# Transposes ahead of the stage borders, stage 3's and 9's preparations too, and adds from VectorE to GpSimd in stage 10, in a twelve-stage perceiver kernel

## What is computed

```python
# stages 3 and 9 (L1_xattn with biases and a mask, L3_xattn without)
qh, kh, vh = proj(q, Wq, bq), proj(k, Wk, bk), proj(v, Wv, bv)   # 16 heads of 8
scores = jnp.where(mask, einsum('bhqd,bhkd->bhqk', qh, kh) / np.sqrt(8), -1e9)
out = einsum('bhqk,bhkd->bhqd', softmax(scores), vh)             # 257 keys
return einsum('bsd,ed->bse', out, Wo) + bo
# stage 8 (L2_ffn): 32 experts x 4 sets, one token of the 32 picked per set
perm = (logits == max(logits, axis=-3))
inner = relu(einsum('bnesd,esdf->bnesf', permuted, W1) + b1)
result_permuted = einsum('bnesf,esdf->bnesd', inner, W2) + b2
# stage 10 (L3_attn): dense 16-head attention and top-6 sparse attention, fused
fused = sig * dense_output + (1.0 - sig) * sparse_output
x = layernorm(src + fused, ln1_g, ln1_b)
ff = relu(x @ ff1_w.T + ff1_b) @ ff2_w.T + ff2_b
return layernorm(x + ff, ln2_g, ln2_b)
```

## Time and profile before

| | |
|---|---|
| runs | 2987.17, 2988.69, 2990.55 (median 2988.69) |
| the profiled execution's own time | 2988.34 |
| its span | 2986.6 |
| mean granted clock | 0.958 |
| busy: PE, DVE, ACT, POOL | 2773.4, 1757.0, 1308.3, 706.8 |
| borders 2 to 3, 8 to 9, 9 to 10, 10 to 11 | 807.8, 1515.6, 1768.8, 1937.7 |

### The profile page before, as it was taken

How to read it: one execution, slowest core, us unless ns; L and a number is a source line. 1 busy time by engine, 2 the same in 40 slices (tenths; PEclk the granted TensorE clock), 3 DMA queues, 4 the chain that set the end, 5 groups by cost and what they waited for, 6 DMA issues and landing times.

```text
span 2986.6 us, 69018 instructions
## 1 busy us (share of the span) xinstructions
PE 2773.4 (93%) x26509; PEld 1781.9 (60%) x26509; DVE 1757.0 (59%) x5682; ACT 1308.3 (44%) x3510; POOL 706.8 (24%) x1552
## 2 busy tenths in 40 slices
PE   8999998997999979998699987699999999999898
PEld 7888885565577756665467755444444444444465
DVE  6787777766478867559568867712232232232544
ACT  4665565552288842358368864311121121111221
POOL 2444441000178830034037751000000000000000
PEclk9999999999999989869889999889999999999999
DMA  5111110000021100410021130030000000000000
GB/s 134 50 48 46 48 41 8 3 3 6 20 55 49 43 25 1 118 60 2 6 58 41 41 133 27 15 126 1 1 1 1 1 1 1 1 1 1 1 1 15
DMA packets 125903, 92.03 MB, mean 31 GB/s; under 512 B 41283, under 2 KB 122566, under 8 KB 124230
## 3 DMA queue, kind: packets, MB, share of 16 engines
q1 hardware_dynamic: 125574, 87.61, 10.3%
HBM read 83.89 MB, written 3.67 MB: 29 GB/s over the span
## 4 chain that ended last, share of the span: by engine, by line
PE 78%; DVE 10%; issue 5%; DVEq 3%; ACT 2%; POOLq 1%; POOL 1%; DMA 0%; SPq 0%; ACTq 0%
PE banks L3558 25%; PE banks L491 3%; PE banks L926 3%; PE banks L897 2%; PE banks L910 2%; PE banks L935 2%; PE banks L3981 2%; PE banks L3972 2%; PE banks L521 2%; PE banks L3970 2%; PE banks L500 2%; PE banks L471 2%; PE banks L508 2%; PE banks L509 2%; PE banks L1759 1%
## 5 line engine op out<-in xcount | busy, mean ns | idle before, releaser
L1011 ACT ACTIVATE probs<-probs,nbias 128x257 f32<-128x257 f32 x512 | 254.3, 501 | 0.0
L1227 POOL TENSOR_SCALAR probs<-probs,rinv 128x257 f32<-128x257 f32 x512 | 237.6, 483 | 25.0 <-DVE rinv L1109 21.8
L3558 PE MATMUL banks<-Wz,hT 128*64 128x256 f32 x2048 | 226.4, 379 | 0.0
L3831 POOL COPY rb<-hT 128x512 f32<-128x512 f32 x32 | 35.8, 1118 | 801.7 <-ACT hT L3634 777.4
L3558 PE MATMUL banks<-Wn,hT 128*64 128x512 f32 x1024 | 225.4, 593 | 0.0
L3558 PE MATMUL banks<-Wr,hT 128*64 128x512 f32 x1024 | 225.2, 592 | 0.0
L3558 PEld LDWEIGHTS banks<-Wz,hT 128*64 128x64 f32 x2048 | 147.0, 137 | 87.7 <-issue 18.3
L3800 DVE TENSOR_TENSOR pr<-hb,banks 128x512 f32<-128x512 f32 x32 | 22.0, 688 | 298.4 <-PE banks L3613 298.4
L717 POOL TENSOR_SCALAR probs<-probs,rinv 128x257 f32<-128x257 f32 x256 | 120.1, 482 | 205.0 <-DVE rinv L657 204.4
L3558 PEld LDWEIGHTS banks<-Wr,hT 128*64 128x64 f32 x1024 | 73.5, 137 | 132.6 <-issue 128.0
L3558 PEld LDWEIGHTS banks<-Wn,hT 128*64 128x64 f32 x1024 | 70.9, 137 | 129.5 <-issue 129.5
(11 more groups left out here) (664 smaller groups left out, 6485.0 us busy)
## 6 DMA issues: line engine op xcount, KB each, us to landing
kvT<-in_ctx_T SPq DMA_DIRECT2D x192, 128.5 KB
kv<-in_ctx SPq DMA_DIRECT2D x64, 128.0 KB
kv<-in_ctx SPq DMA_DIRECT2D x32, 256.0 KB
W<-in_L_ffn_W_T SPq DMA_DIRECT2D x2, 2048.0 KB
Wr<-in_L_ffn_w_hh_T SPq DMA_DIRECT2D x1, 4096.0 KB
Wn<-in_L_ffn_w_hh_T SPq DMA_DIRECT2D x1, 4096.0 KB
Wz<-in_L_ffn_w_hh_T SPq DMA_DIRECT2D x1, 4096.0 KB
v_last<-v_last SPq DMA_DIRECT2D x192, 8.0 KB, 1.6
```

Of the source, the lines that this page charges most:

```text
L1011: i = e.activation(s, s, ACT.Exp, bias=self.nbias[v][:, r:r + 1], scale=self.scale, accum_out=self.rows_sum[v][:, r:r + 1])
L1227: e.tensor_scalar(s, s, self.rinv[v][:, r:r + 1], 1.0, ALU.mult, ALU.mult)
L3558: mm = e.matmul(self.bank[b][hf * BATCH:(hf + 1) * BATCH, 0:n], lhs, rhs, start=start, stop=stop, tile_position=(0, hf * BATCH))
```

## The change

1. The transposes of quarters 0 to 2 and their yT copies go ahead of the barrier in stages 1 to 3 and 5 to 11, in new methods `pe_early` and `act_early`; quarter 3 stays behind it. Banks for them are chosen to be free.
2. Stages 3 and 9: SP issues the first mask and the first four contexts at the end of the previous stage's queue (`sp_early`); POOL makes masks, `wo_heads` (from DVE), `of_batch`, the maps of mask 0 and the last keys of batches 0 and 1 ahead of the barrier (`pool_early`). The products of the last row, keys and values of batches 0 and 1 and the four `v_rows` products with their copies (from DVE to ACT) become eight pieces k = 0 to 7 of `ahead_pe` and `ahead_act`. In stage 3 they stand in `pe_early`, around the transposes and the projection of tile 0. The prologue then runs scores(g - 2) ahead of keys and values g for g = 2 to 5.
3. Stage 9's eight pieces run among the experts of stage 8: PE's piece n // 2 on odd pairs n, in front of `expert_pe`, ACT's piece n // 2 - 2 on even pairs from 4 on. `keep_warm` in `expert_pe` goes.
4. Stage 10: `scale_rows` and `add_x` of every quarter but the last add run on POOL, with new counts x1_scaled, x1_normed and x1_added; DVE does the four softmaxes in a row, then the sparse top and rest. `last_add` fuses the last norm, gain and add.
5. Stage 11's `of_row` is made ahead of the barrier.

```diff
+    def pe_early(self, e):
+        self.norm_pe(e, (0, 1, 2))
+
+    def act_early(self, e):
+        self.norm_act_yT(e, (0, 1, 2))
...
+    def ahead_pe(self, e, k):
+        p, bank = self.prog, self.bank[2 + k % 2]
+        if k == 0:
+            p.constants_made.wait_ge(e, 1)
+            self.weights_wait(e)
+            e.matmul(bank[:, 0:BATCH], self.wk[:, :], self.ctx_last[:, :], start=True, stop=True)
+            e.matmul(bank[:, BATCH:2 * BATCH], self.wv[:, :], self.ctx_last[:, :], start=True, stop=True)
+            i = e.matmul(bank[0:1, P:2 * P], p.ones[0:1, 0:1], self.brow[:, :], start=True, stop=not self.biased)
+            if self.biased:
+                i = e.matmul(bank[0:1, P:2 * P], self.bv[:, :], self.wo[:, :], start=False, stop=True)
+            i.then_inc(self.prep_mm.up(), 1)
+        if k == 1:
+            self.keys_values(e, 0, bank)
+        if k == 2:
+            self.prep_act.wait_ge(e, 3)
+            e.matmul(bank[:, 0:P], p.ones[0:1, :], self.bo_eff[:, :], start=True, stop=True).then_inc(self.prep_mm.up(), 1)
+        if k == 3:
+            self.v_ready.wait_ge(e, 1)
+            self.keys_values(e, 1, bank)
+        if k >= 4:
+            self.wo_ready.wait_ge(e, 1)
+            self.prep_act.wait_ge(e, 4)
+            self.v_ready.wait_ge(e, 2 * (k % 2))
+            self.v_rows_ready.wait_ge(e, k - 5)
+            e.matmul(bank[0:BATCH, :], self.v_lastT[:, :], self.wo_heads[:, (k - 4) * 512:(k - 3) * 512],
+                     start=True, stop=True).then_inc(self.prep_mm.up(), 1)
+
+    def ahead_banks_free(self, e):
+        self.v_rows_ready.wait_ge(e, 4)
+
+    def pe_early(self, e):
+        before = self.prog.stages[self.index - 1]
+        self.x_free = None
+        if not before.RUNS_AHEAD:
+            self.ahead_pe(e, 0)
+            self.ahead_pe(e, 1)
+        self.norm_pe(e, (0, 1))
+        before.last_banks_free(e)
+        self.n_yT.wait_ge(e, 1)
+        self.project(e, 0)
+        self.norm_pe(e, (2,))
+        if not before.RUNS_AHEAD:
+            for k in range(2, 8):
+                self.ahead_pe(e, k)
     def pe(self, e):
-        p, bank = self.prog, self.bank
-        self.norm_pe(e, (0,))
-        self.weights_wait(e)
-        e.matmul(bank[4][:, 0:BATCH], self.wk[:, :], self.ctx_last[:, :], start=True, stop=True).then_inc(self.prep_mm.up(), 1)
-        e.matmul(bank[5][:, 0:BATCH], self.wv[:, :], self.ctx_last[:, :], start=True, stop=True).then_inc(self.prep_mm.up(), 1)
-        i = e.matmul(bank[6][0:1, 0:P], p.ones[0:1, 0:1], self.brow[:, :], start=True, stop=not self.biased)
-        if self.biased:
-            i = e.matmul(bank[6][0:1, 0:P], self.bv[:, :], self.wo[:, :], start=False, stop=True)
-        i.then_inc(self.prep_mm.up(), 1)
-        self.norm_pe(e, (1, 2))
-        self.x_free = None
-        self.n_yT.wait_ge(e, 1)
-        self.prep_act.wait_ge(e, 1)
-        self.project(e, 0)
-        self.prep_act.wait_ge(e, 3)
-        e.matmul(bank[7][:, 0:P], p.ones[0:1, :], self.bo_eff[:, :], start=True, stop=True).then_inc(self.prep_mm.up(), 1)
-        self.keys_values(e, 0)
-        self.norm_pe(e, (3,))
+        self.ahead_banks_free(e)
+        self.n_yT.wait_ge(e, 3)
+        self.prep_pool.wait_ge(e, 1)
+        for g in range(2, 6):
+            self.scores(e, g - 2)
+            self.keys_values(e, g, self.bank[self.X_BANK])
+            if g == 3:
+                self.norm_pe(e, (3,))
+            if g == 4:
+                self.project(e, 1)
         self.n_yT.wait_ge(e, 4)
-        self.prep_act.wait_ge(e, 4)
-        self.prep_pool.wait_ge(e, 1)
-        for g in range(1, 6):
-            self.keys_values(e, g)
-            if g == 5:
-                break
-            self.scores(e, g - 1)
-            if g == 3:
-                self.project(e, 1)
-            if g == 1:
-                self.wo_ready.wait_ge(e, 1)
-                for q in range(3):
-                    self.last_values(e, q)
-            if g == 2:
-                self.v_rows_ready.wait_ge(e, 1)
-                self.last_values(e, 3)
-        self.v_rows_ready.wait_ge(e, 4)
         self.turn_probs(e, 0)
...
+    def act_early(self, e):
+        before = self.prog.stages[self.index - 1]
+        if not before.RUNS_AHEAD:
+            self.ahead_act(e, 0)
+            self.ahead_act(e, 1)
+        self.norm_act_yT(e, (0, 1, 2))
+        if not before.RUNS_AHEAD:
+            for k in range(2, 8):
+                self.ahead_act(e, k)
...
-        p, bank = self.prog, self.bank
-        self.norm_dve_statistics(e)
         self.weights_wait(e)
         self.take_queries(e, 0)
-        self.norm_dve_rows(e)
-        self.head_made.wait_ge(e, 1)
-        e.tensor_tensor(self.wo_heads[:, :].rearrange("p (h d) -> p h d", h=H), self.wo[:, :].unsqueeze(1).to_broadcast([P, H, P]),
-                        self.head_mask[:, :].unsqueeze(2).to_broadcast([P, H, P]), ALU.mult).then_inc(self.wo_ready.up(), 1)
-        p.constants_made.wait_ge(e, 1)
-        e.tensor_reduce(self.of_batch[:, :], p.ident[:, :].rearrange("p (c z b r) -> p z b c r", c=4, z=2, b=BPT)[:, 0], AX.XY, ALU.add)
+        self.norm_dve_statistics(e)
+        self.prep_pool.wait_ge(e, 1)
         for g in range(4):
             self.row_maxes(e, g)
             if g == 0:
-                for q in range(3):
-                    self.take_last_values(e, q)
-            if g == 1:
-                self.take_last_values(e, 3)
-                self.prep_pool.wait_ge(e, 1)
+                self.norm_dve_rows(e)
             if g == 2:
                 self.take_queries(e, 1)
                 self.inverses(e, 0)
...
+        e.tensor_tensor(self.wo_heads[:, :].rearrange("p (h d) -> p h d", h=H), self.wo[:, :].unsqueeze(1).to_broadcast([P, H, P]),
+                        hm[:, :].unsqueeze(2).to_broadcast([P, H, P]), ALU.mult).then_inc(self.wo_ready.up(), 1)
+        of_row = self.ident32[:, 0:BPT * 4].rearrange("p (b r) -> p b r", r=4)
+        e.tensor_tensor(self.of_batch[:, :], of_row[:, :, 0], of_row[:, :, 1], ALU.add)
+        for r in (2, 3):
+            e.drain()
+            e.tensor_tensor(self.of_batch[:, :], self.of_batch[:, :], of_row[:, :, r], ALU.add)
         e.drain().then_inc(self.prep_pool.up(), 1)
         self.map_sink(e, 0)
         self.map_factor(e, 0)
+        self.prep_act.wait_ge(e, 1)
+        self.put_k_last(e, 0)
+        self.put_k_last(e, 1)
+
+    def pool(self, e):
         self.spread_queries(e, 0)
-        self.prep_act.wait_ge(e, 1)
-        for g in range(3):
-            self.put_k_last(e, g)
+        self.put_k_last(e, 2)
...
-    def sp_first(self, e):
+    def sp_early(self, e):
         self.load_mask(e, 0)
         for g in range(self.RING):
...
             if m >= 0:
                 self.norm.start_dve(e, self.s1)
+                self.x1_added.wait_ge(e, m - 1)
                 self.norm.rows_dve(e, self.s1, self.s2[m % 2])
                 e.drain().then_inc(self.s2_normed.up(), 1)
             if r < N:
                 self.add_values(e, r)
                 self.sparse_max(e, r)
-                attn.softmax_dve(e, 4 * r)
-                attn.softmax_dve(e, 4 * r + 1)
-            if m >= 0:
-                self.x1_turned.wait_ge(e, m + 1)
-                self.scale_rows(e, m, self.g1, self.be1)
+                for s in range(4):
+                    attn.softmax_dve(e, 4 * r + s)
+                self.sparse_top(e, r)
+                self.sparse_rest(e, r)
             if m >= 1:
-                self.add_x(e, m - 1)
+                self.x1_added.wait_ge(e, m)
+                self.next_statistics(e, m - 1)
             if r == N:
                 for q in range(3):
                     self.next_rows(e, q)
-            if r < N:
-                self.sparse_top(e, r)
-                attn.softmax_dve(e, 4 * r + 2)
-                attn.softmax_dve(e, 4 * r + 3)
-                self.sparse_rest(e, r)
             if m >= 0:
                 s2 = self.s2[m % 2]
+                self.x1_scaled.wait_ge(e, m + 1)
                 self.w2_mm.wait_ge(e, m + 1)
                 e.tensor_tensor(s2[:, :], bank[self.W2_BANK][:, :], s2[:, :], ALU.add).then_inc(self.s2_ready.up(), 1)
                 e.drain()
...
-            if m >= 0:
+            if 0 <= m < N - 1:
                 self.norm.rows_dve(e, s2, s2)
-                e.drain()
...
-        self.add_x(e, N - 1)
+        self.last_add(e, self.s2[(N - 1) % 2])
+
+    def last_add(self, e, s2):
+        norm, at = self.norm, lambda u: slice(u * P, (u + 1) * P)
+        x = self.prog.X[:, (self.ROUNDS - 1) * R4:self.ROUNDS * R4]
+        for u in range(4):
+            e.scalar_tensor_tensor(s2[:, at(u)], s2[:, at(u)], norm.mv[:, 2 * u:2 * u + 1], self.g2[:, :], ALU.subtract, ALU.mult)
+        norm.std.wait_ge(e, norm.var.count)
+        e.reciprocal(norm.rstd[:, :], norm.rstd[:, :])
+        self.x1_added.wait_ge(e, self.ROUNDS)
+        e.drain()
+        for u in range(4):
```

(31 more changed lines are left out.)

149 lines of the change are left out of this document (81 added, 68 removed).

## The result

| | runs | median | lowest to highest |
|---|---|---|---|
| before | 10 | 2988.36 | 2978.83 to 2994.83 |
| after | 10 | 2979.01 | 2969.32 to 2985.24 |

What follows compares the result with a forecast made beforehand. TensorE, busy 93% of the span, was taken as the bound, with time to win in border ramps and stage 10's rounds. 10.2 + 4.2 - 2.4 + 9.1 + 6.7 = 27.8 us off 2988.3 gave 2961 us; range 2949 to 2975.

Steps and rivals of the forecast that it cites:

- Stage 3's scores: Stage 3 ramp: work moved ahead brings scores(0) to about 817 and turn_probs(0) to 830.5, gaining 4.2 us.
- The stall at 5 to 6: Border of stages 5 to 6: DVE's 2.39 us wait for ScalarE's root of quarter 3 goes, gaining 2.3 us.
- Stage 11's of_row products: Border 10 to 11: with transposes and POOL's of_row ahead, these matmuls start at the border, gaining 2.6 us.
- The plain borders: Transposes moved ahead of ordinary stage borders: 0.7 us at each of four, 10.2 us for all borders together.
- 9 to 10: Border of stages 9 to 10: earlier first projection and fewer transposes before the QK projections, 2.5 us taken.
- The pieces of stage 9 among the experts: Stage 8 expert loop: six of eight pieces overrun the hole by about 0.4 each, losing 2.4 us.
- about 0.85, so I expect it to hold: Stage 8 expert loop without dummies: TensorE's busy share over two pairs is about 0.85, so its 0.99 clock holds.
- rival 3: The clock falls in part of stage 8's expert loop; three five-microsecond stretches lose about 4 us each: 2973 us, 13%.
- land some 2.5 later (an estimate): Stage 9 ramp: contexts go out at 1526.6, land 2.5 us later, turn_probs(0) at about 1533, gaining 9.1 us.
- wo_heads on POOL ... hides in its idle 79 us: POOL's wo_heads multiply, some 5 us by estimate, fits in POOL's idle time ahead of stage 9's border.
- The hold of the port: Stage 10: POOL's operations can hold DVE operations with two SBUF inputs; one hold taken, 1.2 us lost.
- Net 6.7: Stage 10 rounds: norm work moved to POOL and DVE reordered gain 7.9 us, less one 1.2 us hold.

Runs made afterwards that it cites:

- even_warm: Changed kernel with one dummy matmul back on the even expert pairs only; median 2968.10 us, ratio to before 0.9934.
- nodummy: The kernel before, with the one small matmul of each expert pair left out; median 2994.14 us, ratio to before 1.0022.
- both_fixes: Changed kernel with the edits of even_warm and ctx_early together; median 2961.70 us, 2959.77 in a second set of runs.
- ctx_early: Changed kernel with stage 9's contexts of batches 4 and 5 issued ahead of stage 10's weight loads; median 2973.14 us, ratio to before 0.9949.
- late_maps: both_fixes with POOL's preparation of stage 3 held until stage 2's first finished round; median 2955.96 us, 2958.21 in a second set of runs.
- own10: both_fixes with stage 10's layer norm work back on DVE as before the change; median 2972.33 us, ratio to before 0.9952.
- late_turns: both_fixes with transposes and copies of all early-turn stages except 3, 9 and 10 put back behind their borders; median 2981.78 us.
- late_turns_warm: late_turns with a small product in every expert pair and the POOL hold of late_maps; median 2972.23 us, ratio to before 0.9947.
- again: The changed kernel, unaltered, run a second time; median 2983.35 us over 12 runs, ratio to before 0.9978.

## Why the prediction was wrong

**What held.** Most of the places were right. Stage 3's scores came 9.3 after the border for 9.2 and its turn 23.4 for 22.8; the whole stage is 1.6 us shorter in the first trace (259.0 for 260.6). The stall at 5 to 6 went: from the first of quarter 3's statistics to its reciprocal it was 4.4 us (1204.7 to 1209.10) and is 2.0. Stage 11's of_row products start at the border, and the stage is 1.6 us shorter in the first trace for 2.6. The plain borders, 7.7 forecast with that one and without 9 to 10, measured some 6.6 with an error of 3. The pieces of stage 9 among the experts cost what was forecast: with its clock at 1.00 the loop took 27.6 us in even_warm, for 27.5. The rest of stage 8 made up for that: the loop starts 28.2 after the border for 29.3, and from its end to the next border it is 22.0 for 23.8.

**The step that failed: "about 0.85, so I expect it to hold".** I took the loop's clock from an average of busy shares over two pairs. The change takes the small product out of all pairs and puts pieces into every second one, and the clock fell. That was rival 3, at 13%, priced at 12 us; even_warm puts it at 12 to 15 and nodummy shows it with nothing of the change in. It alone is most of the missing 18.5. Its evidence was in the kernel: products that write a bank nobody reads, in a loop whose clock is 0.99, were listed as filler to be removed, and their purpose was a question the trace of before could not answer. The Trainium skill (TensorE: Matmul & The Clock Gate, Part 1) has idle lower the clock; nodummy agrees, with 0.97, 0.72 and 0.50 in three windows, though TensorE was still busy 4.02 and 3.66 of 5 us in the first two. I cited it and still gave it 13%.

**The second: "land some 2.5 later (an estimate), and after keys, scores(3) and copies turn_probs(0) comes at about 1533".** Both sizes were too small. The landing took 4.6, behind a queue of 21 weight loads just issued, and came 1.5 late after the border (15.1 for 13.6). From there to the turn it was 7.3 for 3.9, of which half clock is only some 0.7: at full clock it is 6.6 in both_fixes. The turn came 4.9 later than forecast, and the whole stage gained 3.7 in the first trace for 9.1. ctx_early gives 10.2 for the contexts by the medians, of which its trace explains 4 to 6.

**The third: "wo_heads on POOL ... hides in its idle 79 us".** That is true of stage 9, where I had read the idle time. The same line runs for stage 3 too, at the start of stage 2, where DVE makes the operands of TensorE's next products. The hold of the port, which I had priced in stage 10 (1.2, from a row of 1.43; there it came as three holds of about 0.6, and once 1.1, in the traces of after and both_fixes), came as 3.4 us in one instruction at a place that I did not price: stage 2 is 82.7 us for 76.2, and 76.2 and 75.6 again with late_maps. Nor is stage 8 out of its reach: there POOL's line misses the subtraction of `pick` by 0.9 us in the changed kernel (1446.9 to 1447.8), and holds it in the two kernels whose turns stand behind the border.

**A term on the other side: "Net 6.7" for stage 10.** It was 11.4 to 11.8 by own10. I summed TensorE's waits, less one hold. They are 5.3 of it; the other 6.5 is that the same products took less time, at a mean clock of 0.92 for 0.87. That the clock rises because the waits shrink is my reading; no run has one without the other. DVE is relieved of 11.55 us, close to what the stage lost; one pair of traces does not make a rule of that.

**The sum as measured.** Plain borders 6.6 and stage 10 11.4 are gains by experiment; stage 3 gives 1.6 and stage 9 3.7 by their lengths in the first trace; against them the expert loop's clock, -12.3 to -15.3, and stage 2, -6.5. The 2.4 of the pieces that overrun is made up for within stage 8. That is 1.5 to 4.5, beside 9.3 measured. Several of the terms have errors of 3 us, so the sum closes to 5 us or so and no better; it says which terms are large, and can't say that none is missing.

**What stays open.** When exactly a loop keeps its clock: late_turns fell with TensorE busy 4.83 and 4.98 of 5 us in the windows ahead, nodummy with 4.02 and 3.66, and both_fixes stayed at 1.00. Between both_fixes and late_turns the start of the loop differs (by 10.6 us), and so does the work ahead of it, where the turns stand behind the border and TensorE waits longer for `pick`; I tried neither alone. Whether holding back POOL's preparation is worth anything to the whole kernel is open as well. The fastest versions, late_maps and both_fixes, cannot be told apart; by their ratios each is 25 to 33 us faster than before.

## What to carry to other kernels

A product whose result nobody reads is a part of the design until a run without it says otherwise; before a change takes its place, test the loop without it alone. Putting one back where a piece already fills the hole costs time (2.7 us here). When a helper's work is moved to an earlier stage, price it in every stage where that helper runs, and beside what DVE does there, not in the place where idle time was found. When loads are let through ahead of a border, count the whole queue in front of the last one that the ramp needs, landing included, and the work from its landing to the end of the ramp. An experiment that puts one part of a change back can make it collide with the parts that stay; look in its trace for costs that the kernel before did not have.

## What the runs showed of the hardware that I had not expected

- The granted clock can fall to 0.50 in a loop in which TensorE was busy 3.66 to 4.98 of 5 us in the windows at the fall (nodummy, after, late_turns); at half clock a product of 16 small matmuls goes from 0.67 to 1.13, so a low clock makes the busy share look good. A busy share read at 0.50 says nothing of what it was when the clock fell.
- Which kernels fall can't be read from those busy shares: one filler in two pairs held 1.00 in both_fixes and left 0.50 in late_turns, 18 us apart in stage 8; in late_maps the same filler let the clock dip for a few microseconds.
- A POOL multiply of 3.86 us holds a DVE subtraction of 0.69 for 4.10, and is itself 0.25 longer there (3.61 alone). In late_turns_warm it held a subtraction for 3.95 and was 3.61 long all the same.
- Equal programs differ by 16 us from run to run (22 in `again`: 2968.25 to 2989.92), and a stage by 5 to 8 us between two traces of one program (stage 10 161.5 and 156.1, stage 8 83.8 and 91.8), so a single trace can't size a term under 5 us unless the stage is as steady as stage 2, which stayed within 2.2 us in the eight traces of the changed kernel and its variants without POOL's wait.
